# Expert slots of a token-routing layer: 135 instead of 144, full tiles first, one row region per expert

## The chip, the cores and the metric

The kernel runs on one core of one Trainium2 chip. The metric is the device time of a run in microseconds. The profiler took one execution of the kernel; its rows below are counted from the start of its span.

## The reference, cut to what matters

Tokens x channels is 8192 x 128: eight batches of 1024 tokens. The last of three layers is a mixture of experts with two experts per token.

```python
x = _L0_conv_ref(x, ...)              # attention over 1024 tokens per batch
t = _to_tokens(x)
t = t + _L1_attn_ref(_ln_t(t), ...)   # state-space layer, 8 heads of 32
t = t + _L1_ffn_ref(_ln_t(t), router_w, w1, w2, w3)
...
N_EXPERTS = 8; TOP_K = 2; C, H = 128, 341
probs = softmax(flat @ router_w.T)
topk_probs, topk_idx = top_k(probs, TOP_K)     # gates: the two, normalised
h = silu(h1) * h3                              # h1 = flat @ w1[e].T, h3 = flat @ w3[e].T
out = sum over the two experts of gate * (h @ w2[e].T)
```

## The kernel before, in words

**The two halves of the program.** Until about 766 us the kernel works through 64 tiles of 128 tokens: attention, state-space layer and routing, in steps `step(base, i)`. For each batch of 8 tiles (`NT = 8`) the routing gives every token two row numbers, and GpSimd scatters the normalised rows into the DRAM tensor `xg` (`rows_by_expert`, line 1165), sorted by expert. What follows are the expert slots. A slot is one tile of 128 rows of one expert: SyncE fetches it into `GX` (`fetch`, line 361), TensorE transposes it (`x_T`, line 676), multiplies by W1 and W3 (`hidden`, lines 685 and 690) and by W2 (`result`, line 702), ScalarE applies SiLU and the gate, VectorE copies W3 for the next slot (`weights`, line 1715), multiplies the two hidden halves (`gated`, line 1711) and takes row numbers and gates (`take_gates`, lines 1723 and 1724), and GpSimd scatters the result into `yg` (`results_by_choice`, `put`, line 1054). Line 1711 runs once per slot from slot 13 on and is used below as the clock of the slots; slots are counted from 1, the code's `t + j` from 0. Slots 1 to 12 (`EARLY`) are done inside the steps of the tail of the first half.

**Slots and parts.** An expert's number of rows depends on the data, so the number of slots must be a bound. Before, the batches were split in two parts with row regions of their own: batches 0 to 5 (`SPLIT = 6`) with 2 * 48 + 8 = 104 slots, which can start before the last two batches are routed, and batches 6 and 7 with 2 * 16 + 8 = 40 slots. The + 8 of each part is for one partly filled tile per expert; such a tile is filled up with zero rows (`fill_up`, line 346).

**Tables.** `TBI` holds for each slot its first row and a number that packs the experts of the next slots. The table of the first part is made inside the steps (`table_counts(0)` to `table_rows`), that of the second on VectorE between slots, at `TABLE = {EARLY + 29 + 2 * n: n for n in range(6)}`, that is in the slots t + j = 41, 43, ... 51, behind `take_gates`. Every operation of a table waits for the one before (`Steps.then`). At a slot whose t + j is a multiple of 4 a group begins (`GROUP = 4`), and each engine first loads the packed experts with register instructions (`experts_of`).

**The end.** When all results of a batch are in `yg`, SyncE loads them (`y_load`, line 376: four transfers of 256 KB, two choices by two halves), VectorE adds the two choices and the residual `T2` (`add`, lines 1748 and 1751) and ScalarE's queue stores the sum (`store`, line 969). Batches 0 to 5 need the first 104 slots, and their loads stand on SyncE's queue between the fetches of the last groups; batches 6 and 7 need all slots:

```python
results_written(COUNT[0])
for g in range(TURN + 3, GROUPS):
    fetches(g * GROUP)
    b = g - (TURN + 3)
    if b < SPLIT: ... y_load(b, h)
results_written(SLOTS)
```

What sets the order is thus the written order of each engine's queue and the semaphores. `fetch` of slot n waits until VectorE's `take_gates` of slot n - 4 is done (`dix_ready`), because `GX` has four buffers.

## Time and profile before

| | us |
|---|---|
| three runs | 1157.26, 1159.17, 1159.95; median 1159.17 |
| span of the profiled execution | 1156.2 |
| median less span | 3.0 |
| first and last product of line 1711 | 847.3 and 1135.7 |
| from the last of them to the end of the span | 20.5 |
| TensorE busy | 1052.0 (91%) |

The profiled execution has no time of its own beside its span; the 3.0 us between the span and the median of the runs stand for what lies around it. "Busy" is the time that instructions of an engine occupied it; matmuls are pipelined, so a busy TensorE need not be one at its peak.

### The profile page before, as it was taken

What the parts mean: (1) busy time and instruction counts of PE and PEld (TensorE: products, weight loads), DVE (VectorE), ACT (ScalarE), POOL (GpSimd) and SP (SyncE); (2) the same over time, 40 slices, a digit from 0 to 9 for tenths busy, and PEclk for the clock granted to TensorE, in tenths of its full rate; (3) what the DMA queues carried; (4) which work ended last, traced back from release to release, by engine and by line L of the source; (5) the groups of instructions that cost most, each with busy time, mean ns of one, the idle gap of its engine ahead of it and who ended that gap; (6) DMA issues with size and microseconds to landing.
All of it is one profiled execution on the core that took longest, in us unless ns stands there. A gap on an engine that the chain in (4) does not pass through costs nothing.

```text
span 1156.2 us, 28221 instructions
## 1 busy us (share of the span) xinstructions
PE 1052.0 (91%) x7924; PEld 957.2 (83%) x7924; DVE 840.3 (73%) x3054; ACT 760.0 (66%) x1914; POOL 625.2 (54%) x987
## 2 busy tenths in 40 slices
PE   4889999999999999999999999888889999999993
PEld 3678888888887888888888787777788999999893
DVE  3588888988988888898898888877535554444564
ACT  2677677777767867777776776666556666666551
POOL 8123443467557466656655745654755466444442
PEclk9999999999999999999999999989989999999997
DMA  7300000001000100100100000010112222223566
GB/s 216 72 3 29 12 3 30 7 25 41 10 30 10 41 20 12 48 7 26 40 15 25 9 23 11 16 45 28 42 52 64 65 80 80 78 73 101 169 183 186
DMA packets 66405, 58.66 MB, mean 51 GB/s; under 512 B 12869, under 2 KB 56429, under 8 KB 66253
## 3 DMA queue, kind: packets, MB, share of 16 engines
q1 hardware_dynamic: 48237, 34.54, 10.8%
q0 software_dynamic: 8704, 17.97, 4.7%
q10 hardware_dynamic: 9312, 4.33, 1.4%
q8 instruction: 69, 1.13, 0.4%
q14 instruction: 83, 0.68, 0.2%
HBM read 32.67 MB, written 25.21 MB: 50 GB/s over the span
## 4 chain that ended last, share of the span: by engine, by line
PE 47%; issue 17%; DVE 14%; POOL 12%; ACT 4%; DMA 3%; SPq 2%; DVEq 1%; POOLq 0%; ACTq 0%
PE pY L690 6%; PE pX L685 6%; PE pc L519 5%; PE pa L574 3%; PE pb L702 3%; PE pd L702 3%; DVE CV L1449 2%; PE pY L483 2%; DMA GX<-rows_by_expert 2%; POOL rows_by_expert L1165 2%; POOL YG L1103 2%; POOL st L1146 2%; PE pc L523 1%; POOL STE L1094 1%; PE pX L496 1%
## 5 line engine op out<-in xcount | busy, mean ns | idle before, releaser
L1054 POOL DMA_INDIRECT results_by_choice<-YE,DIX x144 | 144.5, 1003 | 147.3 <-ACT YE L948 120.4
L1165 POOL DMA_INDIRECT rows_by_expert<-XA,SL x128 | 148.1, 1157 | 36.8 <-issue 36.2
L1711 DVE TENSOR_TENSOR V<-XT,pY 128x384 f32<-128x384 f32 x132 | 73.1, 554 | 125.6 <-ACT XT L938 117.8
L519 PEld LDWEIGHTS pc<-XDT,M 128*128 128x128 f32 x1024 | 124.1, 193 | 12.9 <-issue 8.9
L1449 DVE SCALAR_TENSOR_TENSOR CV<-XBC,cw,CV 128x256 f32<-128x256 f32 x288 | 129.9, 505 | 0.0
L574 PE MATMUL pa<-V,PT 128*128 128x128 f32 x1024 | 128.9, 280 | 0.7 <-DVE XDT L1498 0.6
L519 PE MATMUL pc<-XDT,M 128*128 128x64 f32 x1024 | 122.9, 273 | 5.3 <-DVE CT L1455 5.3
L574 PEld LDWEIGHTS pa<-V,PT 128*128 128x128 f32 x1024 | 120.7, 193 | 3.4 <-issue 1.3
L1103 POOL TENSOR_TENSOR YG<-Y,SZ 128x256 f32<-128x256 f32 x64 | 46.4, 725 | 142.5 <-DVE Y L1485 128.8
L1460 DVE TENSOR_REDUCE NM<-pX 128x1 f32<-128x1024 f32 x64 | 78.1, 1220 | 48.7 <-PE pX L498 48.6
L930 ACT ACTIVATE XT<-pa 128x128 f32<-128x128 f32 x132 | 36.5, 277 | 106.4 <-PE pa L676 106.3
L821 ACT ACTIVATE PR<-pX,NM 128x1024 f32<-128x1024 f32 x64 | 71.3, 1114 | 42.8 <-DVE NM L1460 42.7
L792 ACT ACTIVATE PT<-pY 128x1024 f32<-128x1024 f32 x64 | 65.5, 1023 | 42.3 <-PE pY L483 42.3
L1584 DVE TENSOR_TENSOR M<-ED,GT 128x1024 f32<-128x1024 f32 x64 | 78.5, 1226 | 13.4 <-ACT ED L854 13.0
L483 PE MATMUL pY<-ident,PR 128*128 128x128 f32 x512 | 68.4, 277 | 1.5 <-ACT PR L821 1.5
L483 PEld LDWEIGHTS pY<-ident,PR 128*128 128x128 f32 x512 | 60.6, 147 | 5.2 <-ACT PR L821 1.9
L938 ACT ACTIVATE XT<-pX 128x384 f32<-128x384 f32 x132 | 64.0, 485 | 1.1 <-PE pX L685 1.1
L854 ACT ACTIVATE ED<-pY 128x1024 f32<-128x1024 f32 x64 | 64.5, 1008 | 0.0
L1094 POOL TENSOR_TENSOR STE<-ST,ETOT 32x256 f32<-32x256 f32 x56 | 39.1, 698 | 43.7 <-DVE ST L1653 43.6
L496 PE MATMUL pX<-QH 128*128 128x512 f32 x128 | 56.2, 439 | 5.9 <-DVE QL L1209 5.9
L685 PE MATMUL pX<-XT,PR 128*128 128x128 f32 (+1 forms) x396 | 55.6, 277 | 2.8 <-ACT XT L930 2.4
L685 PE MATMUL pX<-XT,X 128*128 128x128 f32 (+1 forms) x396 | 55.4, 276 | 1.4 <-ACT XT L930 1.4
(322 smaller groups left out, 3043.3 us busy)
## 6 DMA issues: line engine op xcount, KB each, us to landing
GX<-rows_by_expert SPq DMA_DIRECT2D x144, 65.0 KB
XT<-in_xT_dram SPq DMA_DIRECT2D x8, 512.0 KB, 4.0
X<-in_x_dram SPq DMA_DIRECT2D x16, 256.0 KB, 3.0
out_dram<-T ACTq DMA_DIRECT2D x16, 256.0 KB
results_by_choice<-YE,DIX POOLq DMA_INDIRECT x144
rows_by_expert<-XA,SL POOLq DMA_INDIRECT x128, 2.6
XBC<-results_by_choice SPq DMA_DIRECT2D x8, 256.0 KB, 3.9
XA<-results_by_choice SPq DMA_DIRECT2D x8, 256.0 KB, 5.0
```

What stands on the lines that cost most here:

```text
L483: last = nc.tensor.transpose(pY[:, P * j:P * j + P], PR[:, P * j:P * j + P], ident[:])
L519: mm(pc[:, 64 * h:64 * h + 64], M[:, h, :], XDT[:, e % 2, HD * h:HD * h + 64], start=h == 0, stop=False, skip_group_check=True)
L574: last = mm(pa[:, 0:C], PT[:, P * j:P * j + P], V[:, j, :], start=j == 0, stop=j == NT - 1)
L685: last = mm(pX[0:hn, 512 * par + P * k:512 * par + P * k + P], WS[par][:, 0, h0:h0 + hn], GXT[par], start=True, stop=True, skip_group_chec ...
L821: A(PR[:], pX[:], ACT.Exp, bias=NM[:, i:i + 1], accum_out=RS[:, i:i + 1]).then_inc(s("exp_ready"), 1)
L1054: g.indirect_dma_start(yg, bass.IndirectOffsetOnAxis(ap=DIX[:, slot, :], axis=0), YE[:, slot, :], None).then_inc(s(f"ye{slot}_scattered"), 16)
L1103: g.tensor_tensor(YG[:], Y2[:], SZ[:, (base + e) // 2 % 3, e % 2, :], ALU.mult).then_inc(s("yg_ready"), 1)
L1165: g.indirect_dma_start(xg, bass.IndirectOffsetOnAxis(ap=SL[:, j // NT, j % NT:j % NT + 1], axis=0), XA[:, j // NT, j % NT, :], None).then_ ...
L1449: return stt(CV[:, m, :], XBC[:, m, fo + tap:fo + tap + 256], cw[:, m, tap:tap + 1], CV[:, m, :], ALU.mult, ALU.add)
L1460: v.tensor_reduce(NM[:, i:i + 1], pX[:], AX.X, ALU.max, negate=True).then_inc(s("nm_ready"), 1)
L1584: tt(M[:], ED[:], GT[:, None, :].broadcast_to([P, H, P]), ALU.mult).then_inc(s("m_ready"), 1)
L1711: tt(HT[par].rearrange("p k t -> p (k t)"), SH[:, par, :], pY[:, 512 * par:512 * par + HP3], ALU.mult).then_inc(s("hh_ready"), 1)
```

## The change

Only the number and order of the slots, their tables and the writing back are changed.

- **One region per expert** of 64 * 128 + 128 rows for all batches, so only one partly filled tile per expert: 2 * 64 + 7 = 135 slots (`SLOTS`).
- **Part one is 88 slots** (`FULL` = 96 - 8), all of them tiles that the first six batches fill completely. It needs no zero rows: the eight `fill_up` transfers before the first fetch go, those of the second part stay.
- **Part two has 47 slots** (`REST`): full tiles of batches 0 to 5 that were left over, then tiles that batch 6 completes, then those that batch 7 completes or leaves open. Its table treats 3 * 8 = 24 segments (`SEGMENTS`), and so the comparison and the two products of the table have 47 * 24 = 1128 elements where two of 40 * 8 = 320 stood. There are seven table functions (`rest_counts` to `rest_digits`) in the slots t + j = 41 to 53 in place of six.
- **Writing back**: after 104 slots batches 0 to 5 can be added up (as before), after 120 batch 6, after 135 batch 7. The loads of batches 0 to 6 stand behind the fetches of groups 27 to 33, and `results_written` is called before each of them.

```diff
@@ -22,13 +22,13 @@
     HC = [(P * k, min(P, HID - P * k)) for k in range(-(-HID // P))]
...
-    REGION = [tiles * P + P for tiles in PARTS]
-    FIRST_ROW = [0, E * REGION[0] + E * P]
-    COUNT = [TOP * tiles + E for tiles in PARTS]
-    FIRST_SLOT = [0, COUNT[0]]
-    SLOTS = sum(COUNT)
-    ROWS = FIRST_ROW[1] + E * REGION[1] + E * P
+    REGION = TILES * P + P
+    ROWS = E * REGION + E * P
+    FULL = TOP * SPLIT * NT - E
+    SLOTS = TOP * TILES + E - 1
+    REST = SLOTS - FULL
+    SEGMENTS = 3 * E
+    SIX_DONE, SEVEN_DONE = TOP * SPLIT * NT + E, TOP * (SPLIT + 1) * NT + E
...
@@ -240,8 +249,8 @@
         PIECES = {FIRST + 1: (TILES, 7), FIRST + 2: (TILES + NT, 0), FIRST + 3: (TILES + NT, 1), FIRST + 4: (TILES + NT, 2), FIRST + 5: (TILES + NT, 3)}
         LATE_ROWS = {GROUP * (FIRST + 6) + 2 * n + 5: n for n in range(TOP * NT)}
         REST_ROWS = {EARLY + 1 + 2 * n: 10 + n for n in range(6)}
-        TABLE = {EARLY + 29 + 2 * n: n for n in range(6)}
-        LEAD, TURN = FIRST + 14, FIRST_SLOT[1] // GROUP - 1
+        TABLE = {EARLY + 29 + 2 * n: n for n in range(7)}
+        FILL, TURN = FIRST + 11, FULL // GROUP - 1
...
+        GROUPS = -(-SLOTS // GROUP)
+        LOADS = SIX_DONE // GROUP + 1
+        ADDS = {LOADS + 2 + b: b for b in range(GROUPS - LOADS - 2)}
         HALF = NT * C // 2
...
             def results_written(slots):
                 for j in range(RESULTS):
-                    sp.wait_ge(s(f"ye{j}_scattered"), 16 // RESULTS * slots)
+                    sp.wait_ge(s(f"ye{j}_scattered"), 16 * ((slots - j + RESULTS - 1) // RESULTS))
...
@@ -375,36 +383,33 @@
                     src = yg[first:first + NT * P, :].rearrange("(p t) c -> p t c", p=P)[:, h * NT // 2:(h + 1) * NT // 2, :]
                     sp.dma_start(Y01[b % len(Y01)][c_][:, h * NT // 2:(h + 1) * NT // 2, :], src).then_inc(s(f"y{b % len(Y01)}{h}_loaded"), 16)
-            sp.wait_ge(s("zt_saved"), 48)
-            fill_up(0, range(E))
             rows_complete(0)
             fetches(0)
             spread_sums(TILES - 4)
             fetches(GROUP)
             spread_sums(TILES - 2)
-            for g in range(2, LEAD + 3):
+            for g in range(2, FILL):
                 fetches(g * GROUP)
-            for g in range(LEAD + 3, LEAD + 7):
+            for g in range(FILL, FILL + 4):
                 for j in range(GROUP):
                     fetch(g * GROUP, j)
                     if j % 2 == 1:
-                        fill_up(1, [2 * (g - LEAD - 3) + j // 2])
-            for g in range(LEAD + 7, TURN + 1):
+                        fill_up([2 * (g - FILL) + j // 2])
+            for g in range(FILL + 4, TURN + 1):
                 fetches(g * GROUP)
             rows_complete(1)
-            for g in (TURN + 1, TURN + 2):
+            for g in range(TURN + 1, LOADS):
                 fetches(g * GROUP)
-            results_written(COUNT[0])
-            for g in range(TURN + 3, GROUPS):
+            for g in range(LOADS, GROUPS):
                 fetches(g * GROUP)
-                b = g - (TURN + 3)
-                if b < SPLIT:
-                    if b >= len(Y01):
-                        sp.wait_ge(s("added"), 2 * (b + 1 - len(Y01)))
-                    for h in range(2):
-                        y_load(b, h)
-            results_written(SLOTS)
-            for b in range(SPLIT, TILES // NT):
+                b = g - LOADS
+                results_written(SIX_DONE if b < SPLIT else SEVEN_DONE)
+                if b >= len(Y01):
+                    sp.wait_ge(s("added"), 2 * (b + 1 - len(Y01)))
+                for h in range(2):
+                    y_load(b, h)
+            for b in range(GROUPS - LOADS, TILES // NT):
+                results_written(SLOTS if b == TILES // NT - 1 else SEVEN_DONE)
                 sp.wait_ge(s("added"), 2 * (b + 1 - len(Y01)))
                 for h in range(2):
...
+            def rest_counts():
+                tables[1] = Steps(dve, "table_steps", 1, 0, 1, 64)
+                then = tables[1].then
+                dve.wait_ge(s("route_steps"), 4 * TILES)
+                dve.wait_ge(s("slots_ready"), TILES)
+                dve.wait_ge(s("off_kept"), 2)
+                ts(ZI[:], OFF, 1.0, None, ALU.add).then_inc(s("zi_ready"), 1)
+                edges = EDGES[:, 1:4, :]
+                then(tt(edges, OFFS[:], ebase[:, None, :].broadcast_to([P, 3, E]), ALU.subtract))
+                then(ts(edges, edges, 1.0 / P, (P - 1) / P - 63.5 / P, ALU.mult, ALU.add))
+                then(v.tensor_copy(EDGEI[:], edges))
+                then(v.tensor_copy(edges, EDGEI[:]))
+                then(ts(MADE[:, 1:], CTE[:], float(FULL), None, ALU.min))
+                then(tt(EDGES[:, 0, :], MADE[:, 1:], MADE[:, 0:E], ALU.subtract))
+            def rest_lengths():
+                then = tables[1].then
+                flat = EDGES[:].rearrange("p k e -> p (k e)")
+                then(tt(LONG[:], flat[:, E:], flat[:, 0:SEGMENTS], ALU.subtract))
+                for k in range(3):
+                    tables[1].did(tt(NT8[:, k], upto8[:], LONG[:, None, k * E:k * E + E].broadcast_to([P, E, E]), ALU.mult))
+                tables[1].settle()
+                then(v.tensor_reduce(ENDS[:].rearrange("p (k e) -> p k e", k=3), NT8[:], AX.X, ALU.add))
+                for k in (1, 2):
+                    then(ts(ENDS[:, k * E:k * E + E], ENDS[:, k * E:k * E + E], ENDS[:, k * E - 1:k * E], None, ALU.add))
+            def rest_starts():
+                then = tables[1].then
+                flat = EDGES[:].rearrange("p k e -> p (k e)")
+                then(tt(START[:, 0:SEGMENTS], flat[:, E:], ENDS[:], ALU.subtract))
+                then(stt(START[:, 0:SEGMENTS], START[:, 0:SEGMENTS], float(P), first_row[:], ALU.mult, ALU.add))
+                then(ts(START[:, SEGMENTS:], ENDS[:, SEGMENTS - 1:], -float(P), float(E * REGION), ALU.mult, ALU.add))
+                then(tt(JUMP[:], START[:, 1:], START[:, 0:SEGMENTS], ALU.subtract))
+            own = itile[:]
+            by = lambda a: a[:, None, :].broadcast_to([P, REST, SEGMENTS])
+            def rest_slots():
+                then = tables[1].then
                 upto(dve, "ydiag_ps", TILES, 0)
-                then(tt(GE, own[:, :, None].broadcast_to([P, n, E]), by(CTE), ALU.is_ge))
-                then(v.tensor_reduce(done, GE, AX.X, ALU.add))
-
...
+            def rest_rows():
+                then = tables[1].then
+                then(tt(GEX, GE, by(JUMP), ALU.mult))
+                then(v.tensor_reduce(TB[:, 0, :], GEX, AX.X, ALU.add))
+                then(ts(TB[:, 1, :], own, float(P), START[:, 0:1], ALU.mult, ALU.add))
+                then(tt(TB[:, 2, :], TB[:, 0, :], TB[:, 1, :], ALU.add))
+            def rest_experts():
+                then = tables[1].then
+                then(tt(GE, GE, by(TURN_), ALU.mult))
+                then(v.tensor_reduce(EXPERT[:, 1 + FULL:1 + SLOTS], GE, AX.X, ALU.add))
+            def rest_digits():
+                then = tables[1].then
+                a, z = TURN * GROUP, SLOTS + 1
                 then(v.tensor_copy(DIGS[:, a:z], EXPERT[:, DIGITS - 1 + a:DIGITS - 1 + z]))
                 for j in range(DIGITS - 2, -1, -1):
                     then(stt(DIGS[:, a:z], DIGS[:, a:z], float(E), EXPERT[:, j + a:j + z], ALU.mult, ALU.add))
-                v.tensor_copy(TBI[:, 0, first:first + n], row)
+                v.tensor_copy(TBI[:, 0, FULL:SLOTS], TB[:, 2, :])
                 then(v.tensor_copy(TBI[:, 1, a:z], DIGS[:, a:z]), True)
                 v.nop().then_inc(s("table_ready"), 1)
...
@@ -1733,7 +1762,7 @@
                     if t // GROUP in ADDS:
                         add(ADDS[t // GROUP], j)
                     if t + j in TABLE:
-                        (table_counts, table_firsts, table_slots, table_tiles, table_experts, table_digits)[TABLE[t + j]](1)
+                        (rest_counts, rest_lengths, rest_starts, rest_slots, rest_rows, rest_experts, rest_digits)[TABLE[t + j]]()
             dve.wait_ge(s("experts_loaded"), 16 * 5)
             dve.wait_ge(s("table_ready"), 1)
             weights(0, experts_of(dve, EARLY)[1])
...
-            for b in range(SPLIT, TILES // NT):
+            for part in range(SLOTS % GROUP, GROUP):
+                add(len(ADDS) - 1, part)
+            for b in range(len(ADDS), TILES // NT):
                 for h in range(2):
                     add(b, h)
                     add(b, h + 2)
```

VectorE, from the last small copy of slot t + j = 47 (before) and 49 (of the change): the table function that follows it. `SX` holds the comparison (`GE`), `XBC` its product, `TB` the table's rows, `X` is a buffer of W3. Before:

```order
L1724 COPY GATE<-GX 128x1
L1408 TENSOR_TENSOR SX<-SX,NTE 128x320
L1409 TENSOR_REDUCE TB<-SX 128x40 [waits table_steps]
L1410 TENSOR_TENSOR TB<-itile,TB 128x40 [waits table_steps]
L226 TENSOR_LOAD TBI [waits table_steps]
L226 ISA x2
L1715 ISA
L1715 COPY X<-W 128x341
L1711 TENSOR_TENSOR V<-XT,pY 128x384 [waits h3_ps,silu_ready]
```

Of the change:

```order
L1753 COPY GATE<-GX 128x1
L1442 TENSOR_TENSOR XBC<-SX,JUMP 128x1128
L1443 TENSOR_REDUCE TB<-XBC 128x47 [waits table_steps]
L1444 TENSOR_SCALAR TB<-itile,START 128x47 [waits table_steps]
L1445 TENSOR_TENSOR TB<-TB 128x47 [waits table_steps]
L1744 ISA [waits table_steps]
L1744 COPY X<-W 128x341
L1740 TENSOR_TENSOR V<-XT,pY 128x384 [waits h3_ps,silu_ready]
L1752 CAST DIX<-GX 128x1 [waits ye2_scattered,gx2_loaded]
```

The two operations have 1128 elements where they had 320, a further small one has joined, and the function stands in a slot with no group behind it, so no `TENSOR_LOAD` follows.

SyncE, the loads of batch 1 behind the last fetch of their group. Before:

```order
L361 ISA [waits dix_ready,gxt_ps]
L361 DMA GX<-rows_by_expert 128x130
L376 DMA ED<-results_by_choice 128x512
L376 DMA M<-results_by_choice 128x512
L376 DMA ED<-results_by_choice 128x512
L376 DMA M<-results_by_choice 128x512
L357 TENSOR_LOAD TBI
L357 ISA x2
L361 ISA [waits dix_ready,gxt_ps]
L361 DMA GX<-rows_by_expert 128x130
```

Of the change:

```order
L369 ISA [waits dix_ready,gxt_ps]
L369 DMA GX<-rows_by_expert 128x130
L384 DMA ED<-results_by_choice 128x512 [waits ye4_scattered,ye5_scattered,ye3_scattered,ye6_scattered,ye2_scattered,ye7_scattered,ye1_scattered,ye0_scattered]
L384 DMA M<-results_by_choice 128x512
L384 DMA ED<-results_by_choice 128x512
L384 DMA M<-results_by_choice 128x512
L365 TENSOR_LOAD TBI
L365 ISA x2
L369 ISA [waits dix_ready,gxt_ps]
L369 DMA GX<-rows_by_expert 128x130
```

Between the fetch and the first load now stand waits for eight semaphores, one for each result buffer; the next fetch still stands behind all four loads.

VectorE, from the last product of the slots on. `ED` belongs to batch 1 and 5, `TR` and `TA` to 2 and 6, `XA` to 3 and 7, `XBC` to 0 and 4. Before:

```order
L1711 TENSOR_TENSOR V<-XT,pY 128x384 [waits h3_ps,silu_ready]
L1723 CAST DIX<-GX 128x1 [waits ye7_scattered,gx3_loaded]
L1724 COPY GATE<-GX 128x1
L1751 TENSOR_TENSOR T<-T,ED 128x512 [waits y_added]
L1748 TENSOR_TENSOR TR<-TR,TA 128x512 [waits y20_loaded]
L1751 TENSOR_TENSOR T<-T,TR 128x512 [waits y_added]
L1748 TENSOR_TENSOR TR<-TR,TA 128x512 [waits y21_loaded]
L1751 TENSOR_TENSOR T<-T,TR 128x512 [waits y_added]
L1748 TENSOR_TENSOR XA<-XA 128x512 [waits y30_loaded]
L1751 TENSOR_TENSOR T<-T,XA 128x512 [waits y_added]
L1748 TENSOR_TENSOR XA<-XA 128x512 [waits y31_loaded]
L1751 TENSOR_TENSOR T<-T,XA 128x512 [waits y_added]
```

Of the change:

```order
L1740 TENSOR_TENSOR V<-XT,pY 128x384 [waits h3_ps,silu_ready]
L1752 CAST DIX<-GX 128x1 [waits ye6_scattered,gx2_loaded]
L1753 COPY GATE<-GX 128x1
L1780 TENSOR_TENSOR T<-T,XBC 128x512 [waits y_added] x2
L1777 TENSOR_TENSOR ED<-ED,M 128x512 [waits y10_loaded]
L1780 TENSOR_TENSOR T<-T,ED 128x512 [waits y_added]
L1777 TENSOR_TENSOR ED<-ED,M 128x512 [waits y11_loaded]
L1780 TENSOR_TENSOR T<-T,ED 128x512 [waits y_added]
L1777 TENSOR_TENSOR TR<-TR,TA 128x512 [waits y20_loaded]
L1780 TENSOR_TENSOR T<-T,TR 128x512 [waits y_added]
L1777 TENSOR_TENSOR TR<-TR,TA 128x512 [waits y21_loaded]
L1780 TENSOR_TENSOR T<-T,TR 128x512 [waits y_added]
```

The additions of batches 4 (its last one) and 5 have joined those of 6 and 7 behind the last slot. Those of batch 7 (`XA`) follow on the piece as four rows more; of all of them they alone need the last slot's results.

## Rows read from the trace of the kernel before

**Rows 1.** The page, part 1: busy us, share of the span, instructions.

```profile
PE 1052.0 (91%) x7924; PEld 957.2 (83%) x7924; DVE 840.3 (73%) x3054; ACT 760.0 (66%) x1914; POOL 625.2 (54%) x987
```

**Rows 2.** Windows: stretch, its us, busy us (count) per engine, clock, DMA share, GB/s.

```profile
1062.44:1135.67 73.23, 68.71 (x609) 67.38 (x609) 43.99 (x150) 41.21 (x127) 34.59 (x32) 1.00 0.57 172
...
1135.67:1156.20 20.53, 1.50 (x12) 1.12 (x10) 6.64 (x12) 0.75 (x3) 3.35 (x4) 0.59 0.73 218
```

**Rows 3.** Line 1711 on VectorE: ns min/median/max, first and last start; slots 56-115, then all.

```profile
L1711 DVE TENSOR_TENSOR V<-XT,pY x60: 553/554/555, 944.3 to 1068.8; 128x384 f32<-128x384 f32 x60
...
L1711 DVE TENSOR_TENSOR V<-XT,pY x132: 532/554/556, 847.3 to 1135.7; 128x384 f32<-128x384 f32 x132
```

**Rows 4.** Timeline of SyncE's queue from 700 us: start, us, what; then its waits.

```profile
754.41 9.56 SPq L346 DMA_DIRECT2D rows_by_expert<-padding_rows  x8
...
768.65 4.13 SPq L361 DMA_DIRECT2D GX<-rows_by_expert  x4
...
SPq L352 <- DMA rows_by_expert<-XA,SL: 3.8, 1, 3.8
```

**Rows 5.** Timeline of VectorE at slots 44 to 54: start, us, what [idle before <-releaser].

```profile
919.10 0.21 DVE L1371 TENSOR_TENSOR NT<-upto,NTE 128x64 f32<-128x64 f32 x1
...
924.56 0.34 DVE L1715 COPY X<-W 128x341 f32 x1 [0.24 <-DVE TB L1401]
...
929.65 0.34 DVE L1715 COPY X<-W 128x341 f32 x1 [0.88 <-DVE TB L1410]
...
935.38 0.56 DVE L1711 TENSOR_TENSOR V<-XT,pY 128x384 f32<-128x384 f32 x1 [1.19 <-ACT XT L938]
...
935.97 0.18 DVE L1426 COPY DIGS<-EXPERT 128x45 f32<-128x45 f32 x1
...
937.49 0.18 DVE L1430 CAST TBI<-DIGS 128x45 int32<-128x45 f32 x1
...
938.67 0.34 DVE L1715 COPY X<-W 128x341 f32 x1 [1.00 <-DVE TBI L1430]
...
940.10 0.55 DVE L1711 TENSOR_TENSOR V<-XT,pY 128x384 f32<-128x384 f32 x1
```

**Rows 6.** The page, part 5: VectorE's product of 1024 elements.

```profile
L1584 DVE TENSOR_TENSOR M<-ED,GT 128x1024 f32<-128x1024 f32 x64 | 78.5, 1226 | 13.4 <-ACT ED L854 13.0
```

**Rows 7.** The chain that ended last, from 1060 us: start, us, what.

```profile
1063.72 0.43 SPq L376
...
1065.57 0.04 issue
...
1065.92 0.15 SPq L357
...
1066.38 3.78 DMA GX<-rows_by_expert
...
1093.38 6.05 DMA GX<-rows_by_expert
...
1104.56 4.24 DMA GX<-rows_by_expert
...
1114.89 2.88 DMA GX<-rows_by_expert
```

**Rows 8.** The same chain from 1136 us to its end.

```profile
1139.36 2.98 DMA results_by_choice<-YE,DIX
...
1143.81 5.55 DMA TA<-results_by_choice
...
1152.77 0.69 DVE T L1751
```

**Rows 9.** The page, part 6: a load's KB and median us from issue to landing.

```profile
XBC<-results_by_choice SPq DMA_DIRECT2D x8, 256.0 KB, 3.9
```

**Rows 10.** Windows around two idle stretches of TensorE; columns as in Rows 2.

```profile
844.00:850.00 6.00, 5.92 (x31) 5.93 (x32) 1.13 (x5) 2.47 (x8) 3.63 (x9) 0.56 0.12 33
...
1096.00:1100.00 4.00, 1.45 (x14) 1.23 (x13) 1.23 (x5) 0.42 (x2) 1.14 (x1) 1.00 0.29 87
```

More of the change, by code:

```diff
@@ L363, in fetches @@
             def fetches(t):
-                for j in range(GROUP):
+                for j in range(min(GROUP, SLOTS - t)):
                     fetch(t, j)
@@ L981, in _ @@
             slot_groups(act, group, between)
-            for j in (2, 1):
-                gate(SLOTS - GROUP, GROUP - j)
-            for b in range(GROUPS - TURN - 6, TILES // NT):
+            for last in (SLOTS - 2, SLOTS - 1):
+                gate(last // GROUP * GROUP, last % GROUP)
+            for b in range(len(ADDS) - 1, TILES // NT):
                 for h in range(2):
@@ L1183, in group @@
             def group(t):
-                for j in range(GROUP):
+                for j in range(min(GROUP, SLOTS - t)):
                     put(t, j)
@@ L1383, in table_columns @@
                 tables[0].did(ts(expert, done, float(E - 1), None, ALU.min))
-                then(stt(row, done, float(REGION[0]), first, ALU.mult, ALU.add), True)
+                then(stt(row, done, float(REGION), first, ALU.mult, ALU.add), True)
             def table_rows():
-                n = COUNT[0]
+                n = FULL
                 dve.wait_ge(s("table_ps"), 1)
@@ L1403, in table_tiles @@
-            def table_tiles(p_):
-                then, n = tables[p_].then, COUNT[p_]
-                by = lambda a: a[:, None, :].broadcast_to([P, n, E])
-                tile, own = TB[:, 1, 0:n], itile[:, 0:n]
-                then(tt(GE, GE, by(NTE), ALU.mult))
-                then(v.tensor_reduce(tile, GE, AX.X, ALU.add))
-                then(tt(tile, own, tile, ALU.subtract))
-            def table_experts(p_):
-                then, n, first = tables[p_].then, COUNT[p_], FIRST_SLOT[p_]
-                done, tile, row = (TB[:, k, 0:n] for k in range(3))
-                then(ts(tile, tile, float(P), float(FIRST_ROW[p_]), ALU.mult, ALU.add))
-                then(stt(row, done, float(REGION[p_]), tile, ALU.mult, ALU.add))
-                then(ts(EXPERT[:, 1 + first:1 + first + n], done, float(E - 1), None, ALU.min))
@@ L1421, in table_digits @@
-            def table_digits(p_):
-                then, n, first = tables[p_].then, COUNT[p_], FIRST_SLOT[p_]
-                row = TB[:, 2, 0:n]
-                a, z = (0, TURN * GROUP) if p_ == 0 else (TURN * GROUP, SLOTS + 1)
+            def rest_counts():
[12 more added lines that the diff above has]
+                then(tt(EDGES[:, 0, :], MADE[:, 1:], MADE[:, 0:E], ALU.subtract))
```

122 lines of the change are left out of this document (58 added, 64 removed).

## The prediction

> **What bounds the kernel now.** I read the page first: TensorE is busy for 91% of the span, every other engine for less [rows 1]. That share hides three stages, so I then took line 1711, which runs once per slot, as a clock. Slots 56 to 115 start from 944.3 to 1068.8 us, 59 intervals in 124.5 us, that is 2.11 us each; its two starts around the table function below are 4.72 us apart for two slots, so the clock shows every disturbance [rows 3, 5]. In the quiet slots nothing but TensorE's own work sets the pace. All 132 products from slot 13 on lie between 847.3 and 1135.7 us [rows 3].
>
> Then the windows. From slot 112 (1062.44) to slot 144 (1135.67) the kernel takes 73.23 us; 32 x 2.11 are 67.5, so **5.7 us are lost** there, and TensorE is busy for only 68.71 [rows 2]. The chain of waits says why: behind the last fetch of a group SyncE issues four loads (the first at 1063.72, end of the four at 1065.57), reads the next slot's row number, and only at 1066.38 issues the next fetch, which lands 3.78 us later, behind 1 MB of its own queue. Six such fetches stand in the chain, each behind the loads of one batch; the first, fourth, fifth and sixth are shown, 2.88 to 6.05 us long [rows 7]. Last, the 20.53 us behind the last product belong to the results: scatter, load, add, store [rows 2, 8].
>
> **The change part by part.**
>
> *Nine slots fewer.* All of them are slots behind the twelfth, in a stage where a slot costs TensorE 2.11 us: 9 x 2.11 = **-19.0 us**. The nine transposes, copies, fetches and scatters go too; they lie beside TensorE.
>
> *The first table and the first zero rows.* The eight zero-row transfers (754.41 to 763.97) no longer precede the first fetch. But that fetch starts at 768.65, and SyncE's last wait before it is for a scatter of rows, 3.8 us [rows 4]. The scatter is still there, so: nothing. If that cover were gone, at most the 3.8 us could be had, since only what SyncE waits for last can be. Shorter tables of 88 columns are a few hundredths. The second part's zero rows move from slots 80 to 95 to slots 56 to 71, both behind fetches with four slots of lead: nothing.
>
> *The second table.* It is made on VectorE between slots, and what is late next is the copy of W3, for which TensorE waits. How much room is there? The digits function starts at 935.97 and ends at 937.67 (1.70 us, eight small operations, 0.21 each); the copy of W3 follows after 1.00 us. The products before and after are 940.10 - 935.38 = 4.72 apart instead of 4.22, so 0.50 us were lost and the room is 1.70 + 1.00 - 0.50 = 2.20 us [rows 5]. The wait behind a function is 0.24 us inside a group, and 0.88 where a group begins and registers are loaded [rows 5]. A product of 64 elements takes 0.21 us and one of 1024 takes 1.226 [rows 5, 6]: 1.06 ns per element, so 1.34 for 1128 and 1.38 from start to start; I give the reduction the same. Then:
> - rest_lengths (slot 43, a group follows): five small, a reduction of 192 (0.39), and a seventh operation, 1.77 + 0.88 = 2.65, loss 0.45
> - rest_slots (47, a group follows): 1.38 + 0.88 = 2.26, loss 0.06
> - rest_rows (49): 2 x 1.38 + 2 x 0.21 + 0.24 = 3.42, loss 1.22
> - rest_experts (51, a group follows): 2 x 1.38 + 0.88 = 3.64, loss 1.44
> - rest_counts, rest_starts, rest_digits: 1.1 to 2.0, within the room.
>
> Together 3.2, less the 0.5 of before: **+2.7 us**. Bounds: +1.5 if wide operations overlap their waits, +4 if each step costs 0.2 more. The late `take_gates` also delays the fetch of four slots on by some 2.2 us, of which TensorE is 1.2 late itself.
>
> *The loads between fetches.* The six disturbed fetches of before come back one group earlier with the same four loads ahead of each. The load of batch 6 stands behind the last fetch of all, so it delays none. New are waits for eight semaphores before each burst, long satisfied, yet in the chain above. No row has one alone. The nearest are the pieces called issue, 0.04 us, and a pair of register instructions, 0.15 [rows 7]. So 0 to 0.1 us each; I take 0.05, as the shorter piece is the more like: 8 x 0.05 x 6 = **+2.4 us** (0 to 4.8). The next fetch is issued later by it and nothing covers that, since the chain runs through it.
>
> *The end.* Before, two batches had to be loaded after the last scatter. From the last product on: the scatter lands at +6.7 (1139.36 + 2.98); the first batch's second half is issued at +8.1 and lands 5.55 us later, behind and before other loads; then six operations follow each other, the last ends at 1153.46, 2.74 us before the end of the span [rows 8]. Of the change only batch 7 is loaded, at the same offsets. Its second half lands at +8.1 plus 3.9, the median of such a load into `XBC` [rows 9], to 5.55. But the stores of batches 4, 5 and 6, 1.6 MB, now fall into the same time with the 1.05 MB: at the 218 GB/s of that window 12.0 us from about +1.7, so +13.7 [rows 2]. I take +13.3, then two additions of 0.69 and 2.74 for the last store: +17.4 against +20.5, **-3.1 us** (-1.5 to -4.4; 0 if the stores block the scatter as well).
>
> The Trainium skill (DMA: Bandwidth & Descriptors, Anatomy of one DMA) fits a transfer as 2.0 us plus its bytes at 436 GB/s. For 256 KB that is an estimate of 2.6 us, where the row shows 5.55; by it the end would come at about +14.9, and the sum would be 2.5 us lower.
>
> *Sum*: -19.0 + 2.7 + 2.4 - 3.1 = -17.0 us. Against the profiled span: 1156.2 - 17.0 = 1139.2. The median of the runs lies 3.0 us above that span, so **1142.2 us**.
>
> **The rivals.**
> - *Bursts weigh less* (15 in 100). The fourth fetch, 6.05 us where its neighbours take 2.9 to 4.2, may have met something that does not come back when everything is shifted (-2.1), and satisfied waits may be free (-2.4): 1137.7. For it: only one of six rows is that long. Against: the same loads into the same buffer meet the same queue.
> - *Bursts weigh more* (15 in 100). If each of the six fetches takes 6.05 us, they cost about 6 x 2.7 = 16 instead of 5.7: 1153. Batch 6's loads and more stores fall into the last slots; against it, the stores begin where they began, relative to the loads.
> - *Not faster at all* (2 in 100): SyncE's waits. They stand between two fetches 48 times, in six places where nothing covers them. Everything but them gives -19.4; so at 0.40 us each the time is that of before, at 0.45 it is 1161.4. The rows beside them, 0.04 and 0.15, speak against it [rows 7].
> - *The clock falls* (2 in 100). From 844 to 850 TensorE ran at a mean granted clock of 0.56, so mostly at the lower of its levels (1.2 and 2.4 GHz), after idling; from 1096 to 1100 it idled for 2.55 us and the clock stayed at 1.00 [rows 10]. The new losses of 1.2 and 1.4 us are shorter than that. If it fell after both, each slot at the lower level costs up to 2.1 us more, some 3 us each time: 1148. The Trainium skill (TensorE: Matmul & The Clock Gate, Part 1) says that the gate has two rates and that idling brings the lower; the trace agrees at 844 and not at 1096.
>
> That the slots don't get fewer is excluded: the bound is a constant.
>
> **How the numbers follow.** The forecast has 66 in 100: its terms give 1139.8 to 1144.6 with one bound at a time, 1137.3 with all low and 1147.5 with all high. To leave out two in ten I go to **1137.5 to 1148**. A measurement tells 0.2% (2.3 us) from no change. Only the SyncE rival ends above 1156.9: slower 0.02, same 0.01, faster 0.97.
>
> **What the profile would show.** 123 products of line 1740, last slot near 1122 us; quiet slots still 2.11 apart; gaps of about 4.2 and 4.5 us in place of 2.11 ahead of slots 51 and 53, each followed by a shorter one, with VectorE's copy of W3 named; 1128-element operations of 1.34 us; six fetches of 3 to 6 us in the chain and, between the last fetch of a group and its first load, some 0.4 us that were not there; from the last product to the end about 17.4 us, with one pair of loads in the chain. The prediction is wrong if that piece is over 0.8 us, if a burst now disturbs more than one slot, or if the stores of batches 4 to 6 delay the last scatter.

## The result and the profile after

The changed kernel takes **1138.51 us** (median of 4 runs, 1138.15 to 1141.22) against 1158.22 of the kernel before, run beside it (4 runs, 1156.86 to 1159.95): ratio 0.9828, 95% interval 0.9804 to 0.9851, or 19.7 us less. The forecast was 17.0 us less. The profiled execution took 1138.55, its span is 1136.7 us.

First the page of the changed kernel, part 1, as in [rows 1]:

```profile
PE 1035.1 (91%) x7753; PEld 938.6 (83%) x7753; DVE 840.3 (74%) x3025; ACT 747.4 (66%) x1878; POOL 616.2 (54%) x983
```

TensorE works 16.9 us less, ScalarE and GpSimd 12.6 and 9.0 us less, VectorE as long as before. TensorE has still the largest share and still bounds. Line 1711 has become line 1740. This is its row in the changed kernel, for all slots from 13 on, as the second of [rows 3]:

```profile
L1740 DVE TENSOR_TENSOR V<-XT,pY x123: 534/554/556, 848.0 to 1119.1; 128x384 f32<-128x384 f32 x123
```

123 products in 271.1 us, where there were 132 in 288.4. With 2.109 us for a slot (the 59 quiet intervals of [rows 3] with one digit more), 9 x 2.109 = 19.0 us are gone, but these stretches differ by 17.3 only. The windows of the changed kernel tell the last slots from the end, as [rows 2] (columns: stretch, its us, busy us and count of PE, PEld, DVE, ACT, POOL, clock, DMA share, GB/s):

```profile
1058.10:1119.14 61.04, 58.17 (x515) 56.88 (x514) 36.23 (x125) 34.60 (x107) 28.73 (x27) 1.00 0.67 204
1119.14:1136.70 17.56, 1.50 (x12) 1.12 (x10) 9.73 (x17) 0.75 (x3) 3.34 (x4) 0.61 0.77 225
```

From slot 108 to the last, 27 intervals take 61.04 us; 27 x 2.109 are 56.94, so 4.1 us are lost to the bursts, where 5.7 were. The end has shrunk from 20.53 us to 17.56. At the table function both kernels differ most. VectorE's timeline of the changed kernel, from the function behind slot 48 to slot 57 (start us, us, engine, line, operation, elements, idle before):

```profile
928.75 1.32 DVE L1437 TENSOR_TENSOR SX<-itile,ENDS 128x1128 f32<-128x1128 f32 x1
930.95 0.34 DVE L1744 COPY X<-W 128x341 f32 x1 [0.88 <-DVE SX L1437]
...
932.38 0.55 DVE L1740 TENSOR_TENSOR V<-XT,pY 128x384 f32<-128x384 f32 x1
...
932.98 1.32 DVE L1442 TENSOR_TENSOR XBC<-SX,JUMP 128x1128 f32<-128x1128 f32 x1
934.34 1.33 DVE L1443 TENSOR_REDUCE TB<-XBC 128x47 f32<-128x1128 f32 x1
...
936.43 0.34 DVE L1744 COPY X<-W 128x341 f32 x1 [0.24 <-DVE TB L1445]
...
937.86 0.56 DVE L1740 TENSOR_TENSOR V<-XT,pY 128x384 f32<-128x384 f32 x1
...
943.46 0.55 DVE L1740 TENSOR_TENSOR V<-XT,pY 128x384 f32<-128x384 f32 x1 [0.26 <-PE pY L695]
...
944.05 0.23 DVE L1457 COPY DIGS<-EXPERT 128x52 f32<-128x52 f32 x1
...
945.73 0.18 DVE L1461 CAST TBI<-DIGS 128x52 int32<-128x52 f32 x1
946.59 0.34 DVE L1744 COPY X<-W 128x341 f32 x1 [0.68 <-DVE TBI L1461]
...
948.02 0.56 DVE L1740 TENSOR_TENSOR V<-XT,pY 128x384 f32<-128x384 f32 x1 [0.26 <-PE pY L695]
...
950.53 0.55 DVE L1740 TENSOR_TENSOR V<-XT,pY 128x384 f32<-128x384 f32 x1 [1.16 <-ACT XT L943]
```

Two slots should take 4.22 us. From 932.38 to 937.86 are 5.48, a loss of 1.26 (forecast 1.22, rest_rows); from 937.86 to 943.46 are 5.60, a loss of 1.38 (forecast 1.44, rest_experts); from 943.46 to 948.02 are 4.56, a loss of 0.34, and the next slot takes 2.51, a loss of 0.40 (forecast for both: nothing). The gaps ahead of slots 51 and 53 were 4.30 and 4.42 us long, as the forecast had it (4.2 and 4.5). With 0.48 at rest_lengths and 0.01 at rest_slots the table loses 3.9 us, against 0.5 before.

The chain that ended last, changed kernel, from the end of the fetch group of the third burst on, and then its last part (a burst is the four loads of one batch; columns: start us, us, what):

```profile
1076.97 0.34 SPq L369
1077.31 0.05 issue
...
1077.60 0.33 SPq L384
...
1080.20 3.96 DMA GX<-rows_by_expert
...
1087.68 1.55 SPq L384
...
1090.58 3.08 DMA GX<-rows_by_expert
...
1098.98 3.89 DMA GX<-rows_by_expert
...
1122.82 3.15 DMA results_by_choice<-YE,DIX
...
1126.55 4.65 DMA XA<-results_by_choice
```

Between the last fetch (1076.97 + 0.34 = 1077.31) and the first load (1077.60) lie 0.29 us: the waits for eight semaphores. The fetches behind the loads that stand in this chain take 2.7 to 4.0 us, none the 6.05 of [rows 7].

The whole difference of the spans, from these rows: start of slot 13's product +0.7, nine slots -19.0, table +3.4, bursts -1.6, end -3.0, together -19.5 us (1156.2 to 1136.7).

### The profile page after: what moved, and what is told of

The parts are those of the page before. It is cut to its first block, busy times and chain, and to the rows that moved or that the text cites. A ratio compares the mean times of both kernels' runs of the same rounds, so it can differ in the third digit from the quotient of the medians.

```text
span 1136.7 us, 27603 instructions
## 1 busy us (share of the span) xinstructions
PE 1035.1 (91%) x7753; PEld 938.6 (83%) x7753; DVE 840.3 (74%) x3025; ACT 747.4 (66%) x1878; POOL 616.2 (54%) x983
## 4 chain that ended last, share of the span: by engine, by line
PE 47%; issue 18%; DVE 14%; POOL 11%; ACT 5%; DMA 2%; SPq 1%; DVEq 1%; ACTq 0%; POOLq 0%
PE pY L695 6%; PE pX L690 6%; PE pc L524 5%; PE pa L579 3%; PE pd L707 3%; PE pb L707 3%; PE pY L488 2%; DVE CV L1480 2%; POOL rows_by_expert L1173 2%; POOL YG L1111 2%; PE pc L528 2%; POOL st L1154 1%; PE pX L429 1%; PE pX L501 1%; PE pa L535 1%
## 5 line engine op out<-in xcount | busy, mean ns | idle before, releaser
L1062 POOL DMA_INDIRECT results_by_choice<-YE,DIX x135 | 135.6, 1004 | 137.0 <-ACT YE L953 109.2
L1740 DVE TENSOR_TENSOR V<-XT,pY 128x384 f32<-128x384 f32 x123 | 68.1, 554 | 112.4 <-ACT XT L943 104.6
L935 ACT ACTIVATE XT<-pa 128x128 f32<-128x128 f32 x123 | 34.0, 276 | 101.6 <-PE pa L681 101.3
L943 ACT ACTIVATE XT<-pX 128x384 f32<-128x384 f32 x123 | 59.7, 485 | 1.1 <-PE pX L690 1.1
L1117 POOL TENSOR_TENSOR XW<-XDT,DEC 128x256 f32<-128x256 f32 x64 | 39.5, 618 | 27.9 <-DVE XDT L1529 27.6
L690 PE MATMUL pX<-XT,PR 128*128 128x128 f32 x372 | 51.7, 275 | 3.1 <-ACT XT L935 2.4
```

The costliest lines, as they stand in the source:

```text
L690: last = mm(pX[0:hn, 512 * par + P * k:512 * par + P * k + P], WS[par][:, 0, h0:h0 + hn], GXT[par], start=True, stop=True, skip_group_chec ...
L1062: g.indirect_dma_start(yg, bass.IndirectOffsetOnAxis(ap=DIX[:, slot, :], axis=0), YE[:, slot, :], None).then_inc(s(f"ye{slot}_scattered"), 16)
```

## The experiments

Runs of one kernel taken together spread over 3 to 8 us, so terms of 1 or 2 us are read from the traces and not from the medians. "Burst loss" is the time of the last 27 intervals between products (32 in the layout of before, from slot 112 on), less 2.109 us each; "table loss" is the same for slots 41 to 57, or to 67 where the table has twelve functions.

### The kernel before once more: how steady are its bursts?

No edit. 

> The kernel before, unchanged, profiled a second time, to see what of its trace repeats. Theory 1 (the long landing belongs to the program: same loads, same buffers, same queue): from slot 112 to slot 144 again 5.7 us are lost against 2.11 us a slot, and the fourth fetch behind a burst of loads again takes about 6 us to land. Rival (it was an accident of that execution): the loss is 3.5 to 4.5 us and no fetch behind a burst takes over 4.5 us; then the loads weigh no less in the changed kernel than before, and the profile of before was merely unlucky by 1 to 2 us.

One execution of 1156.5 us, span 1154.7; nine further runs of the same kernel had a median of 1157.08. Its windows, at the places of [rows 2]:

```profile
1062.51:1134.97 72.46, 68.76 (x610) 67.47 (x609) 44.00 (x150) 41.21 (x127) 34.55 (x32) 1.00 0.58 174
1134.97:1154.70 19.73, 1.49 (x12) 1.12 (x10) 6.64 (x12) 0.75 (x3) 3.34 (x4) 0.61 0.74 226
```

And of its chain the fourth burst:

```profile
1090.01 0.34 SPq L361
1090.39 0.43 SPq L376
...
1093.13 5.11 DMA GX<-rows_by_expert
```

Burst loss 72.46 - 67.49 = 5.0 us where [rows 2] gave 5.7, end 19.73 where it was 20.53. Without the waits the first load stands 0.04 us behind the fetch. The fetch behind the fourth burst is again the longest, but 0.9 us shorter, and neither theory holds in full. A single profile fixes the bursts and the end to no better than about 0.8 us each.

### The changed kernel twice more

No edit, five runs each.

> The changed kernel, unchanged, profiled and timed again. Both theories: 17 to 20 us faster than before. Theory 1 (the loss belongs to the program): from slot 108 to slot 135 again 4.1 us lost, the first burst 1.1 and the second none. Rival (accident): the losses fall on other bursts and sum to anything from 3 to 6 us. The table again costs 3.9 us against 0.5 under both.

1138.22 us (1136.52 to 1140.98), ratio 0.9837 (0.9823 to 0.9852), span 1139.2. The six bursts lost 0.8, 0.5, 0.8, 1.1, 1.4 and 0.5 us, where the first profile had 1.1, 0.0, 0.8, 1.1, 0.8 and 0.2: part of the loss is an accident of the execution, as the rival has it.

> The changed kernel once more, on the chip of the run with both edits, for the comparison; 1138 to 1140 if the kernel before is at 1157 to 1159. Its span again made of 3.9 us lost in the table, 4 to 5.5 us in the bursts and 17.6 us behind the last product.

1138.54 us (1133.43 to 1140.52), ratio 0.9825 (0.980 to 0.985), span 1138.8. Over the three profiles the burst loss is 4.1, 5.5 and 4.4 us, mean 4.6, against 5.7 and 5.0 of before, mean 5.4: by these means the bursts became lighter by about 0.8 us, where the forecast had them 2.4 heavier. Two further kernels below have the same six bursts and lost 5.2 and 3.5 us, so the range of the new layout, 3.5 to 5.5, overlaps that of the old one, 5.0 to 5.7. That they are no heavier is shown, that they are lighter only likely. The table loss is 3.9 in all three and the end 17.6 to 17.8, so these two terms are steady. The profiled executions took 1.7 to 1.9 us more than their spans, not 3.0.

### What the eight waits cost: once, as they are, three times

The waits are written for the first batch that needs them alone, or each three times:

```diff
-                results_written(SIX_DONE if b < SPLIT else SEVEN_DONE)
+                if b in (0, SPLIT):
+                    results_written(SIX_DONE if b < SPLIT else SEVEN_DONE)
```

```diff
-                results_written(SIX_DONE if b < SPLIT else SEVEN_DONE)
+                for _ in range(3):
+                    results_written(SIX_DONE if b < SPLIT else SEVEN_DONE)
```

> The changed kernel with the waits for all eight result buffers only before the loads of batch 0, of batch 6 and of batch 7, so 8 waits fewer in front of five bursts. In the changed kernel's trace the piece from the end of the last fetch's issue to the first load's is 0.29 us where it was 0.05. Theory (the chain runs through SyncE): 0.24 us gained for each burst whose next fetch is late, four or five, so 1.0 to 1.2 us faster than the changed kernel. Rival (queue-bound: the next fetch waits for the megabyte of loads, and its landing does not move with its issue): nothing, within 0.3 us.

> The changed kernel with the eight waits before each burst written three times. Theory (each satisfied wait costs 0.03 us of SyncE and the chain runs through it): the piece between the last fetch and the first load grows from 0.29 to about 0.77 us, and with four to six late fetches the kernel is 2 to 3 us slower than the changed kernel. Rival (queue-bound): unchanged within 0.5 us. If repeated waits are dropped when the program is built, the piece stays at 0.29 us and the run tells nothing.

Once: 1137.64 us (1135.70 to 1139.31), ratio 0.9826 (0.9812 to 0.9839), burst loss 2.8 us. Three times: 1139.66 (1138.34 to 1143.42), ratio 0.9855 (0.9836 to 0.9875), burst loss 8.0 us. The chain of the kernel with three times the waits, at the third burst:

```profile
1075.59 0.34 SPq L369
1075.93 0.05 issue
...
1076.67 0.04 issue
1076.71 0.33 SPq L384
```

From 1075.93 to 1076.71 are 0.78 us for 24 waits, against 0.29 for 8 and 0.04 for none: **0.03 us a wait**, not 0.05. Of the burst loss, 2.8, 4.6 and 8.0 us with one, six and 18 sets of eight waits ahead of a fetch give 5.2 / 17 = 0.31 us a set, a little over the 0.25 of the piece itself. Both put the six sets at 1.5 to 1.8 us; that is rather an upper bound, as the load behind the waits is issued in 0.33 us and the one without them in 0.43. The medians go the same way, by 2.0 us in all, less than half of what the single traces say: once was 0.6 us faster than the changed kernel (forecast 1.0 to 1.2), three times 1.4 slower (forecast 2 to 3). The waits do cost something, and the rival "SyncE's waits, 0.40 each" is dead by a factor of 13.

### The waits in the kernel before

```diff
+                    results_written(COUNT[0])
                     if b >= len(Y01):
```

> The kernel before with one part of the change alone: waits for all eight result buffers before each of its six bursts of loads. Asked is why the six bursts of the changed kernel lose no more (4.1, 5.5 and 4.4 us in three profiles) than those of before (5.8 and 5.0), though the waits were added. Theory (each wait adds 0.03 us to the chain): from slot 111 to 144 the loss is 6.2 to 7.2 us and the kernel 1.2 to 1.5 us slower than before, in so few rounds hardly to be told. Rival (the waits are hidden by the queue): 5.0 to 5.8 as without them.

1160.77 us (1156.75 to 1164.55) against 1158.96, ratio 1.0017 (0.9996 to 1.0038), span 1158.0, burst loss 6.7 us against 5.4 (mean of two). The waits add 1.3 us here in the trace; the median leans that way, and its interval takes in no change. So the trace agrees with the forecast's mechanism, and the changed kernel's bursts seem to have become lighter by something else: 6.7 with the waits in the old layout (one profile), 3.5 to 5.5 in the new one (five profiles).

### The burst one group later

If the new position of the bursts made them lighter, or took away something at the first one, moving them shows it. All loads of batches 0 to 6 stand one group later, so batch 6's pair has no fetch behind its own.

```diff
-        LOADS = SIX_DONE // GROUP + 1
+        LOADS = SIX_DONE // GROUP + 2
```

> The changed kernel with the bursts one group of slots later: batch 0 behind the fetches of group 28, as in the kernel before, and so on, so that batch 5 stands behind the last fetch and batch 6 behind it. Five bursts instead of six have a fetch behind them. Theory (each burst with a fetch behind it costs the same, some 0.8 us): 0.8 us less lost, 3.3 to 4.5 us, and the end as long as before, 17.5 us, since all other additions are done before batch 7 arrives: 0.8 us faster than the changed kernel. Rival (the first burst of the changed kernel is disturbed by the scatters just before it: its four issues took 2.3 to 3.3 us where the first of before took 1.85): later by a group it takes 1.9 us again and the first loss falls from 0.6 to 1.1 to about 0.4, 1.2 us faster in all.

1137.21 us (1135.84 to 1141.80), ratio 0.9826 (0.9797 to 0.9855), span 1138.8, burst loss 4.3 us. The four issues of the first burst took 1.8 us instead of the changed kernel's 2.3 to 3.3 (four profiles of it and its near variants), as expected; but the first burst still lost 0.7 us (the rival said 0.4), and the end grew by 2.1 us, which neither theory nor rival has. The window behind the last product of this kernel, and its chain at the fourth burst and behind the last product:

```profile
1119.12:1138.80 19.68, 1.49 (x12) 1.11 (x10) 12.41 (x21) 0.75 (x3) 3.33 (x4) 0.65 0.89 278
```

```profile
1097.09 5.55 DMA GX<-rows_by_expert
...
1122.79 4.77 DMA results_by_choice<-YE,DIX
...
1129.42 5.14 DMA XA<-results_by_choice
```

With batch 5's loads and additions and more stores in the same time the last scatter needs 4.77 us where it needed 3.15: an effect like the one that the forecast gave as its lower bound ("0 if the stores block the scatter as well") exists, one group away from the change. Which of the loads and the stores does it was not separated.

The chain also shows what moving the bursts brings back. The loads of batch 3, the fourth burst, stand behind the fetches of group 31 again, as in the kernel before. The fetch behind them again takes 5.55 us (6.05, 5.11 and 5.06 in the three profiles of the old layout) and this burst loses 2.4 us. One group earlier, in the changed kernel and its variants, the same fetch took 2.8 to 4.1 us in all eight profiles that have this burst there. So the place of the bursts matters for the fourth one. The 4.3 us, moreover, are the loss of five bursts and not of six. What stands in the way at that place was not traced.

### The end with two batches, as before

```diff
+                if b == SPLIT:
+                    break
...
-            for b in range(GROUPS - LOADS, TILES // NT):
-                results_written(SLOTS if b == TILES // NT - 1 else SEVEN_DONE)
+            for b in range(SPLIT, TILES // NT):
+                results_written(SLOTS)
```

> The changed kernel, but batch 6 is loaded only when all 135 slots are written, as before the change; batch 7 behind it. Theory (the end is a chain of last scatter, loads, additions, last store, and its length goes with the loads behind the last scatter): from the last product to the end of the span 20.5 us as before in place of 17.5, so 3 us slower than the changed kernel, about 1141. Rival (the end is bound by the bytes of stores and loads together, which are the same in both): within 1 us of the changed kernel.

1142.52 us (1140.89 to 1142.83), ratio 0.9861 (0.9829 to 0.9892), burst loss 5.2 us. The window behind its last product, batch 6 loaded after all slots:

```profile
1120.26:1141.10 20.84, 1.49 (x12) 1.11 (x10) 9.83 (x17) 0.75 (x3) 3.33 (x4) 0.64 0.80 239
```

20.84 us against 17.6: the early batch 6 is worth 3.2 us, the forecast's 3.1 (20.5 against 17.4).

### The nine slots alone

`SLOTS` back to 144, in the new layout; the nine slots added hold zero rows only, and the table has 56 columns with them in its second part. The zero rows for them and the two places of the loads that follow from the number are not shown.

```diff
-    SLOTS = TOP * TILES + E - 1
+    SLOTS = TOP * TILES + E - 1 + 9
```

> The changed kernel with nine slots more (144, a table of 56 slots and 1344 elements), which find only rows of zeros and write to padding; so the number of slots is that of before and everything else is the change's. Theory (a slot costs TensorE's 2.11 us whatever it holds, and nothing else of the change has this size): 19.0 us slower than the changed kernel plus 0.8 for the longer table (0.22 us for each of the four large operations that count), so 1157.5 to 1158.5, at or above the kernel before. Rival (fewer bytes at the end or one region per expert bring part of the gain): 1150 to 1155.

1156.49 us (1155.13 to 1158.32), ratio 0.9988 (0.9972 to 1.0005), span 1155.2. Table loss 5.2 us (56 columns are 1344 elements wide), 4.4 us lost in the last 36 intervals, which hold seven bursts here, end:

```profile
1139.04:1155.20 16.16, 1.49 (x12) 1.11 (x10) 3.95 (x8) 0.64 (x3) 3.33 (x4) 0.61 0.58 178
```

That is 1.0 us below the forecast: the table cost 1.3 us more and not 0.8, and the end is 1.4 us shorter than the changed kernel's, since VectorE does 8 operations in it instead of 17. Against the changed kernel's medians of 1138.2 and 1138.5, 18.0 to 18.3 us come back with nine slots, and without them 1.3 us are left of the gain, which the interval of the ratio does not tell from none. The order and the regions by themselves are worth nothing that these runs can tell: what the end gives, the table takes.

### Two improvements: the table in twelve steps, the loads one by one

The losses left suggest two edits. First, no wide operation shares a slot with another: seven functions become twelve.

```diff
-        TABLE = {EARLY + 29 + 2 * n: n for n in range(7)}
+        TABLE = {EARLY + 29 + 2 * n: n for n in range(12)}
...
                 then(tt(GEX, GE, by(JUMP), ALU.mult))
+            def rest_jumps():
+                then = tables[1].then
                 then(v.tensor_reduce(TB[:, 0, :], GEX, AX.X, ALU.add))
```

> The changed kernel with the seven table functions cut into twelve, in the slots 41, 43 to 63, so that no slot has more than one operation of 1128 elements behind it. Theory (a function costs what its duration and the wait behind it exceed 2.20 us): one large operation and its wait are 1.6 us inside a group and 2.26 before a group, so three functions lose 0.06 each and the rest nothing; between slot 41 and slot 65 0.2 to 0.5 us are lost in place of 3.9, and the kernel is 3.4 to 3.7 us faster, 1134.6. Rival (VectorE has no room at all in these slots and lost time is only moved): the same 3.9 us are lost over more slots.

1135.36 us (1131.11 to 1136.78), ratio 0.9796 (0.9769 to 0.9822). VectorE's timeline of this kernel, around its first wide operation:

```profile
933.67 1.32 DVE L1441 TENSOR_TENSOR SX<-itile,ENDS 128x1128 f32<-128x1128 f32 x1
935.23 0.34 DVE L1767 COPY X<-W 128x341 f32 x1 [0.24 <-DVE SX L1441]
...
937.29 0.55 DVE L1763 TENSOR_TENSOR V<-XT,pY 128x384 f32<-128x384 f32 x1 [0.89 <-ACT XT L943]
```

VectorE is idle again before line 1763, waiting for ScalarE and not late itself. The table loss, over all twelve functions, is under 0.1 us (forecast 0.2 to 0.5) instead of 3.9. Second, one load of a batch behind each single fetch instead of four behind a group, and the waits written once:

```diff
+            for g in range(LOADS + 1, GROUPS):
+                b = g - LOADS - 1
+                for j in range(min(GROUP, SLOTS - g * GROUP)):
+                    fetch(g * GROUP, j)
...
+                    y_load(b, j // 2, [j % 2])
```

> The changed kernel with one load of 256 KB behind each fetch of groups 28 to 33 in place of four behind the last fetch of groups 27 to 32, and the eight waits written three times in all. Theory (a fetch is late because it stands behind 1 MB of its own queue and 1.9 us of issues): behind 256 KB and 0.5 us it lands well before it is needed; of the 4 to 5.5 us lost from slot 107 on at most 1 is left, 4 us faster, about 1134. Rival (the loads and the fetches share bandwidth, not a queue): the loss is the same, spread over 24 slots.

1132.98 us (1129.66 to 1137.95), ratio 0.9791 (0.9761 to 0.9821). SyncE's queue in this kernel's timeline and the window of its last 27 intervals:

```profile
1066.51 0.34 SPq L369 DMA_DIRECT2D GX<-rows_by_expert  x1
1066.90 0.43 SPq L384 DMA_DIRECT2D ED<-results_by_choice  x1
1068.62 0.34 SPq L369 DMA_DIRECT2D GX<-rows_by_expert  x1
1069.01 0.43 SPq L384 DMA_DIRECT2D M<-results_by_choice  x1
```

```profile
1055.07:1112.93 57.86, 57.54 (x515) 57.06 (x514) 36.16 (x125) 34.61 (x107) 28.66 (x27) 1.00 0.72 209
```

In these rows the fetches go out every 2.11 us, the pace of a slot. 57.86 us instead of 61.04: 0.9 us lost (57.86 - 56.94) where the changed kernel loses 4.1 to 5.5. Not all of it is the single loads: with the waits written once and the bursts kept, the loss was 2.8 us. By these single traces the waits account for some 1.8 us and the single loads for some 1.9.

The fetches do not land faster for it. In this kernel the 23 fetches from 1057 to 1112 us landed 1.9 to 3.9 us after their issue, 3.4 in the median, no sooner than some behind four loads (2.7 to 4.0 in the chain of the changed kernel). What the edit took away is the delay of their issue. The rival, that the same loss is spread over 24 slots, is refuted. Both edits together:

> The changed kernel with both edits of the last two runs: table in twelve functions and one load behind each fetch. Theory (the two losses are independent, 3.9 us of the table and 4.1 to 5.5 of the bursts): 7 to 8 us faster than the changed kernel, 1130 to 1131; from slot 41 on less than 1.5 us lost in all. Rival (one hides part of the other): 5 us or less.

**1130.10 us** (1127.12 to 1133.75) against 1157.15, ratio 0.9758 (0.9732 to 0.9784); losses under 0.1 and 1.2 us. This is the fastest version, some 8 us under the changed kernel.

## Why the prediction was right

The kernel became faster by 19.7 us where 17.0 was forecast. 1138.5 lies inside the range, but 3.7 us under the point and only 1.0 us above the lower end. The main term and the end were right in mechanism and size; for the bursts the forecast of 2.4 us more was wrong, they cost no more than before, and there its rival "bursts weigh less" (1137.7, 15 in 100) was nearer than its point.

- **Nine slots, -19.0**: right. Quiet slots stay 2.11 us apart, and giving the slots back costs the gain (18.0 to 18.3 us).
- **First table and zero rows, nothing**: the first product of slot 13 starts at 845.8 to 850.7 us in kernels that are alike up to there, before included (847.3 and 847.4). No effect shows; one of 1 or 2 us could hide in that.
- **Second table, +2.7**: measured +3.4 (3.9 against 0.5). rest_lengths, rest_slots, rest_rows and rest_experts were forecast at 0.45, 0.06, 1.22 and 1.44 and cost 0.48, 0.01, 1.26 and 1.38. The first of these agrees by luck: its own terms (six small operations and 0.39) give 1.65 us and not 1.77, so a loss of 0.33, and the trace has 1.68 us, but a wait of 0.99 and not 0.88. What was off is rest_digits. The text compared its length (1.1 to 2.0) with the room of 2.20 us, while that room counts the wait behind a function too: 1.86 + 0.68 = 2.54, loss 0.34, and 0.40 more ahead of slot 57, where a group begins; why it begins later there than at other groups was not tested. By the forecast's own measure of before (1.70 + 1.00 against 2.20) it should have been there.
- **The loads between fetches, +2.4**: this is the term that was mis-sized: -0.8 by the means of three and two profiles. Two parts. The waits cost 0.03 us each, not 0.05: 0.25 us a burst, at most 1.5 to 1.8 us in all. And the six fetches did not lose what they lost before: 4.6 us with the waits, where the old layout with the same waits loses 6.7. The forecast had named this as a rival ("the fourth fetch may have met something that does not come back"), and for that fetch it came: the fourth burst lost 2.8, 1.8 and 1.9 us in the old layout and 1.1, 1.1 and 1.8 in the new (2.1 and 1.1 in the two further profiles). That makes 0.7 to 0.9 of the 2.1 us on the mean; the rest is spread over bursts whose losses vary by 0.5 us and more from profile to profile. One group later the fetch behind the fourth burst took 5.55 us again and the burst lost 2.4, so for it the place goes with the loss. Why that place is worse, and whether the other bursts are lighter at all, stays open.
- **The end, -3.1**: right: 17.6 us behind the last product, forecast 17.4; 3.2 us when undone. The last load landed 4.65 us after its issue, inside the 3.9 to 5.55 of [rows 8, 9]. The last scatter took 3.15 us, and 3.1 to 3.4 in eight further profiles with 135 slots (all but the one with its bursts a group later), where three profiles of the old layout have 2.98, 2.27 and 2.93: a small delay of the kind that the prediction named as a sign against it is there. By the Trainium skill (DMA: Bandwidth & Descriptors, Anatomy of one DMA) the estimate was 2.6 us and the end 14.9; the page fits that formula to transfers issued by GpSimd, and for this load on SyncE's queue, with three other loads and the stores under way, the trace does not agree.
- **From span to median, +3.0**: 1.8 in the later executions; 1.2 us of the miss are this. The profiled execution of before had been faster than the median of its runs, and that was carried over.
- Together, for the profiled execution: the bursts came out 4.0 us under their term, the span to the median 1.2, and the table, the start of slot 13 and the end 0.7, 0.7 and 0.1 over theirs: 3.7 us under the point.
- **The other rivals**: waits of 0.40 us fell (0.03). The clock did not fall behind the table's gaps: it reads 1.00 from 908 to 955 us of the changed kernel and from slot 108 on, and the quiet slots between keep 2.11 us. The prediction counted the idle stretch at 1096 us against the rule that it cites; but the Trainium skill (TensorE: Matmul & The Clock Gate, Part 1) does not say that every idle stretch brings the lower level, so the 1.00 there does not speak against it.

## What to carry to other kernels

Where one engine sets the pace of a uniform stage, the number of its steps is the gain, and the order around them only moves a few microseconds from one place to another. Bookkeeping on another engine is free as long as each piece, with the wait behind it, fits the room of one step: cut it by width, not by meaning (3.8 us here). A small transfer that the next step needs should not be held up by a burst of large loads, and their waits, on one queue; one load behind each fetch, with the waits written once, took 3.7 us out of the stage, about half of it by the waits. The small transfers landed no sooner; they were issued on time.

## What the hardware showed that was not expected

- A satisfied semaphore wait on SyncE costs 0.03 us, and 24 of them 0.78 with the start of the next issue.
- Issuing a load of 256 KB takes 0.43 us on SyncE's queue as a rule, but single issues took 1.2 to 1.6 us (1.55 at 1087.68 in the chain above); a fetch of the next slot then starts that much later.
- A fetch of 65 KB lands 1.8 us after its issue as the median of all 135 in the kernel with single loads, most of which have no load near them; 3.4 us as the median of the 23 that have one load of 256 KB between each and the next; and 2.7 to 6.05 us behind four such loads.
- The last scatter landed after 3.15 us in the changed kernel and 4.77 when more loads and stores fell into its time (278 GB/s in that window against 225); with fewer, in the kernel of 144 slots in the new layout, it took 2.23 (178 GB/s).
